# An attention and feed-forward block on one core: when GpSimd adds the residual's bias, where the next input's statistics stand, and which softmax sums VectorE takes

## What is computed

```python
x = x + jnp.tanh(g_xattn[0]) * xattn(_layernorm(x, axis=-1), ctx_2048, wq, bq, wkv, bkv, wp, bp)
x = x + jnp.tanh(g_ffn[0]) * ffn(_layernorm(x, axis=-1), gate_w, up_w, down_w, gate_scale, up_scale, down_scale)
...
q = _qdq(x) @ _qdq(wq).T + bq
kv = cond @ wkv.T + bkv
attn = jax.nn.softmax(jnp.einsum('bnhd,bmhd->bhnm', q, k) * scale, axis=-1)
o = jnp.einsum('bhnm,bmhd->bnhd', attn, v).reshape(B, N, C)
out = _qdq(o) @ _qdq(wp).T + bp
```

## Time and profile before

| | |
|---|---|
| median of three runs | 938.24 us (937.95 to 938.37) |
| the profiled execution, its own time | 936.7 us |
| its span in the profile | 934.9 us |
| PE busy | 864.1 us, 92% |
| DVE busy | 671.5 us, 72% |
| ACT busy | 554.4 us, 59% |
| POOL busy | 256.7 us, 27% |
| granted TensorE clock, mean | 0.991 |

### The profile page before, as it was taken

The page is one execution under the profiler, slowest core; times in us unless marked ns, Lnnn a source line. Parts: engine busy times, 40 slices in busy tenths (PEclk is TensorE's granted clock), DMA queues, the critical chain, the costliest instruction groups (busy, mean ns, idle before and its releaser), DMA issues.

```text
span 934.9 us, 13575 instructions
## 1 busy us (share of the span) xinstructions
PE 864.1 (92%) x5000; PEld 310.2 (33%) x5000; DVE 671.5 (72%) x1292; ACT 554.4 (59%) x693; POOL 256.7 (27%) x236
## 2 busy tenths in 40 slices
PE   5987888999899998999899998999999989998998
PEld 2421121124433331224433331224433322233443
DVE  6887968938676769876766679886867768678222
ACT  5546777562556657884356647885256678871330
POOL 1145789770017603000006713000001213000130
PEclk9998999999999999999999999999999999999999
DMA  9334244410111143200020133210020014200001
GB/s 332 97 89 128 84 125 116 127 46 1 43 32 46 40 125 96 51 2 1 17 58 24 50 109 97 49 32 1 4 48 1 1 46 111 54 1 23 12 1 45
DMA packets 37106, 55.28 MB, mean 59 GB/s; under 512 B 8944, under 2 KB 15152, under 8 KB 37040
## 3 DMA queue, kind: packets, MB, share of 16 engines
q1 hardware_dynamic: 35120, 48.13, 18.1%
q0 software_dynamic: 1920, 6.29, 2.3%
HBM read 31.21 MB, written 4.19 MB: 38 GB/s over the span
## 4 chain that ended last, share of the span: by engine, by line
PE 68%; DVE 13%; ACT 10%; issue 7%; DMA 1%; ACTq 0%; DVEq 0%
PE ps L1325 33%; PE ps L1469 9%; PE ps L1506 8%; PE ps L1486 8%; ACT r L836 5%; PE ps L1448 4%; DVE acc L1080 3%; PE ps L1500 2%; PE ps L1514 1%; PE ps L1309 1%; DVE kst L1055 1%; ACT xq L795 1%; ACT r L795 1%; ACT r L744 1%; DVE r L1222 1%
## 5 line engine op out<-in xcount | busy, mean ns | idle before, releaser
L836 ACT ACTIVATE r<-ps 128x1024 f32<-128x1024 f32 x256 | 251.4, 1022 | 74.1 <-PE ps L1469 71.7
L1469 PE MATMUL ps<-qst,kst 97*128 97x512 f16 x512 | 140.9, 387 | 15.4 <-ACT r L836 13.0
L1055 DVE CUSTOM_DVE_ANT_0 kst<-ps,kst 128x512 f32<-128x512 f32 x192 | 124.5, 686 | 30.3 <-PE ps L1448 28.4
L1486 PE MATMUL ps<-r,vv 128*32 128x512 f32 x1024 | 138.1, 612 | 3.4 <-ACT r L836 3.2
L1080 DVE TENSOR_TENSOR acc<-acc,r 128x1024 f32<-128x1024 f32 x108 | 129.8, 1258 | 3.5 <-ACT r L836 3.1
L795 ACT ACTIVATE kst<-ps 128x1024 f32<-128x1024 f32 x96 | 98.2, 1023 | 53.3 <-PE ps L1381 53.0
L644 POOL TENSOR_TENSOR rstd<-mv,mhalf 128x4 f32<-128x4 f32 x8 | 9.9, 1240 | 344.9 <-DVE mv L966 344.9
L1325 PE MATMUL ps<-xs,w_gate 128*128 128x512 f16 x384 | 91.0, 380 | 1.5 <-DVE xs L1260 1.5
L1325 PE MATMUL ps<-xs,w_up 128*128 128x512 f16 x384 | 91.1, 380 | 0.0
L1469 PEld LDWEIGHTS ps<-qst,kst 97*128 97x128 f16 x512 | 37.6, 98 | 157.4 <-ACT r L836 110.7
L893 ACT ACTIVATE qst<-ps,gs_c 128x512 f32<-128x512 f32 x48 | 33.0, 688 | 67.7 <-PE ps L1325 67.7
(11 more groups left out here) (164 smaller groups left out, 1322.1 us busy)
## 6 DMA issues: line engine op xcount, KB each, us to landing
kst<-k_reg SPq DMA_DIRECT2D x192, 64.0 KB
qst<-q_reg SPq DMA_DIRECT2D x192, 32.0 KB
xs<-in_x SPq DMA_DIRECT2D x4, 1024.0 KB, 6.0
cf<-in_ctxT POOLq DMA_DIRECT2D x16, 256.0 KB, 3.5
xres<-in_x SPq DMA_DIRECT2D x3, 1024.0 KB, 5.4
out<-xres SPq DMA_DIRECT2D x12, 256.0 KB, 2.1
acc<-in_down_w SPq DMA_DIRECT2D x10, 256.0 KB, 2.6
vv<-in_wkvT SPq DMA_DIRECT2D x2, 1024.0 KB, 9.8
```

The lines of the kernel that those rows point to most:

```text
L836: nc.scalar.activation(prob[:, s:s + 2, :], ps[:, first_bank:first_bank + 2, :], ACT.Exp, scale=SCALE).then_inc(exp_done, 1)
L1055: ins = nc.vector.tensor_tensor_reduce(kept(b, n)[:, k, :], bank(PAIR + k), kept(b, n)[:, k, :], 1.0, -3.0e38, ALU.add, ALU.max, mx[:, g % ...
L1469: mm = nc.tensor.matmul(bank(first_bank + k), kst[0:97, g % 2, j + k, t * P:(t + 1) * P], qst[0:97, g % 2, j + k, :], start=True, stop=True)
L1486: mm = nc.tensor.matmul(ps[j * DH:(j + 1) * DH, O_BANK, :], vv[:, t, h * DH:(h + 1) * DH], prob[:, p_slot(b, u, j), :], start=(t == 0), st ...
```

## The change

Three things change. First, for inputs 1 to 3, POOL waits for `den_out` of the same input, which ACT gives behind the last unit, before it adds the bias. Second, of the steps of `x_ahead(2)` and `x_ahead(3)` the four of statistics no longer stand ahead of units 1 to 4 of the following input: two stand beside `DOWN3`, ahead of the last turned maxima, and two behind the last `down_tile`. The step that puts them together moves from unit 5 to unit 3. Third, `ADDED` is now 0 to 6 in all four groups; before, units 11 and 19 had their sums on PE. DVE so covers 28 units of an input where it covered 26, with 24 units' adds where there were 22.

```diff
-AHEAD_UNITS = ((3, 5, 7, 18, 20) + tuple(range(22, 30)), tuple(range(1, 6)) + tuple(range(8, 25)))
+
+AHEAD_UNITS = ((3, 5, 7, 18, 20) + tuple(range(22, 30)), (3,) + tuple(range(8, 25)))
+AHEAD_EARLY = (2, 2)
...
-ADDED = ((0, 1, 2, 3, 4, 5, 6), (0, 1, 2, 4, 5, 6), (0, 1, 2, 4, 5, 6), (0, 1, 2, 3, 4, 5, 6))
+ADDED = (tuple(range(MT - 1)),) * G
...
                     if b < B - 1:
                         inverse_deviation(variance_of_x(b + 1))
+                    pool.wait_ge(den_out, b + 1)
                     residual_bias(b)
...
-                ahead = x_ahead(b + 1) if not last else None
+                if b == 0:
+                    ahead = x_ahead(1)
...
+                ahead = x_ahead(b + 2) if b + 2 < B else None
                 for t in range(NT):
                     name = f"DOWN{t}"
                     if name not in d_seq(b):
                         continue
-                    beside(name)
+                    for part in AHEAD[b].get(name, []):
+                        if part == [("S", G - 1, 0)] and ahead:
+                            for _ in range(AHEAD_EARLY[0]):
+                                next(ahead)
+                        maxima(b + 1, part)
                     down_tile(b, t, b, name)
+                for _ in range(AHEAD_EARLY[1] if ahead else 0):
+                    next(ahead)
```

## The result

| | before | after |
|---|---|---|
| median | 938.31 us (937.95 to 938.67, 4 runs) | 927.22 us (927.07 to 929.05, 4 runs) |
| ratio | | 0.9888, 95% interval 0.9874 to 0.9902 |
| profiled execution, its own time | 936.7 us | 927.18 us |
| its span | 934.9 us | 925.4 us |
| mean granted TensorE clock in it | 0.991 | 0.994 |

The changed kernel is 1.1% faster, 11.1 us from median to median. The two profiled executions lie only 9.5 us apart; where the other 1.6 us come from is taken up under the clock, further down.

A forecast was written before the change was run, and what follows sets the result against it. PE, in step with ACT, was taken to set the pace, waiting 3.43 us for DVE in inputs 1 and 2. Gains of 3.97 us each there and 1.74 in input 3 made 9.68: 938.24 - 9.7 = 928.5 us, range 925.5 to 932.0.

The forecast's parts named there:

- First group: Inputs 1 and 2: with three statistics and the bias gone, PE's wait goes whole and `totals` comes 3.60 us earlier.
- The spare 0.4 us: First group's end, inputs 1 and 2: `totals` could start at 360.86, PE is ready only at 361.29.
- That both parts are needed: First group's end: with bias or statistics moved alone, PE would still wait for the other, 1.4 us or 1.8 us.
- Second and third group: Inputs 1 and 2: DVE wants 19.43 and 18.41 us against PE's 17.43, giving new waits of 2.00 and 0.98.
- the third rival: The change only moves the wait: each step costs some 0.4 us more inside the adds; 936.5 us, chance 0.06.
- Fourth group and input 3: Fourth group: 16.59 us before and after. Input 3: PE's 17.43 sets the pace, two `sums` of 0.87 come out, 1.74.
- What was costed at nothing: Bias behind the units (no collision, at most 0.4 us) and two statistics beside `DOWN3`, in DVE's idle 1.68 us.
- the first rival: The clock falls in the second group, behind the 2.00 us wait; 929.7 to 931.7 us, chance 0.18.
- The mis-sized term: Last step of the sum: the runs' median lies 1.5 us above the profiled execution, so 938.24 is the starting point.
- the price of the fall: Second group, inputs 1 and 2: the clock at half speed behind the first wait lengthens the distance by 1.61 us.

The follow-up runs named there:

- bias_only: The kernel before, with one edit: POOL waits for `den_out` ahead of the bias of inputs 1 to 3; 930.34 us, ratio 0.992.
- without_sums: The changed kernel with `ADDED` as before the change, so the sums of units 11 and 19 are back on PE; 927.85 us, ratio 0.9892.
- added_only: The kernel before, with only the sums changed: DVE adds units 11 and 19 too in inputs 1 to 3; 937.43 us, ratio 0.9995.
- stats_only: The kernel before, with only the early statistics and the new `AHEAD_UNITS`, the bias as it was; 939.65 us, ratio 1.0014.
- bias_at_scaling: The changed kernel, with the bias waiting for the freed bank of O3 in place of `den_out`; 935.28 us, ratio 0.9968.

## Why the prediction was right, point by point

- **First group:** 3.60 us each were forecast. `totals` came 3.29 us earlier in input 1 (364.89 to 361.60) in an execution that was already 0.3 us behind ahead of the units (the wait of the earlier trace rows at 104.03 stands at 104.32), so 3.6. The spare 0.4 us was not there in input 1: DVE's first add came at 347.33, 0.4 us later than forecast even so, and its last ended 0.06 before `totals`. The delay comes with the early statistics: in all six runs that have them this add starts 3.3 us after ACT's first exponential, in the others 3.0. Why is open; input 2 of the changed kernel has 3.0.
- **That both parts are needed** was right for the wait to go whole, wrong for what each does alone. The bias alone leaves 1.27 us, near the 1.4. The statistics alone don't leave 1.8: the wait is 4.14 us in input 1 and 2.73 in input 2, since the bias follows the variance in POOL's queue. The text ahead of the prediction names that queue, and the prediction doesn't ask what an earlier variance would start.
- **Second and third group:** 19.43 and 18.41 were forecast, 19.31 and 18.41 measured. The 0.12 is the last normalising, which I had taken at 0.58. In the kernel before, a reduction stands right behind it, and `x_ahead` lets no reduction start before all four normalisings have ended (`dve.wait_ge(xn_ready, ...)`); now a unit's adds stand between, and it costs 0.46 like the others (369.45 to 369.91). So the third rival's support, a step that costs more inside the adds, was misread. Waits forecast 2.00 and 0.98, measured 1.66 (1.38 in input 2) and 0.77 as the profile counts them, from the end of the matmul before.
- **Fourth group and input 3:** 16.59 and 17.43 forecast, 16.61 and 17.44 measured.
- **What was costed at nothing** cost nothing, but for the late first add above. The bias took 4.96 us, and L1226 beside it kept its 0.68. The two statistics beside `DOWN3` shortened DVE's idle time there from 1.68 to 0.48 us, and the turned maxima weren't late. The Trainium skill (SBUF, "Who interferes with whom") agrees with the runs in both directions: products from PSUM and reductions go free, scalings and adds within SBUF collide.
- **The clock** stayed at 1.00 behind the new waits of 1.66 and 1.38 us, so the first rival didn't come.
- **The mis-sized term** is the last one, "the median of the runs shown lies 1.5 above that execution". Against the profiled execution 927.0 was forecast and 927.18 measured; that they meet to 0.2 us is in part luck, since by distances the gain is 9.8 and the execution happened to be 0.3 us late ahead of the units. But the 1.5 doesn't carry over: the changed kernel's median is its profiled time. I had taken the price of the fall (1.61 us, from one execution) as fixed. Runs of the kernel before beside their mean granted clock show that it isn't:

```
us        clock
935.24    0.993
936.55    0.991
938.65    0.989
940.30    0.987
```

Each step of 0.002 in the clock goes with some 1.7 us (1.3 to 2.1). It is about what one stretch of 3.4 us at half the clock takes off the mean: half of 3.4 over 935 is 0.0018. The kernel before has three long waits (two of 3.43 us, and one of 2.56 near the end, which all versions here keep), and around each of them the clock may be low for 3.4 or for 6.8 us. The last one can also pass without a fall; the same wait of 2.55 us, the matmuls behind it in two versions:

```profile
857.30:864.10 6.80, 4.81 (x30) 3.08 (x31) 3.64 (x6) 2.74 (x5) 0.00 (x0) 1.00 0.10 39
855.00:861.80 6.80, 5.30 (x17) 2.46 (x16) 2.69 (x5) 1.99 (x5) 0.00 (x0) 0.50 0.10 39
```

The first row is `bias_only`, the second `without_sums`. Counted in stretches of 3.4 us around these three waits, the traces have none in `bias_only` (mean clock 0.996), one in the changed kernel (0.994), two in `without_sums` (0.993), three in the kernel before (0.991), four in `added_only` (0.989) and five in `stats_only` (0.987). The median run of the kernel before had 0.989, which by this count is one stretch more than its profiled execution, and that accounts for the 1.6 us (11.1 less 9.5). At which of the three waits it lay isn't seen in an execution without a trace.

Of the gain, by distances: the bias's place 7.5 us (in each of two inputs 2.16 off the first wait and some 1.57 off the distance behind it), the statistics on top of it 2.9 (the distance from input 1's fourth `totals` to input 2's first goes from 159.41 in `bias_only` to 157.97 in `without_sums`), and the sums lose 0.5: 1.7 gained in input 3 and 2.2 given back in inputs 1 and 2. That is 9.8 us (the terms are rounded), and the 9.5 of the profiled executions is this less the 0.3 us of lateness. The medians (938.10 for the kernel before beside these runs, then 930.34, 927.85, 927.22) say 7.8, 2.5 and 0.6 gained for the same three, with the clock's falls mixed in.

## What to carry to other kernels

Cost an edit in the unit in which two engines meet (here from `totals` to `totals`), once for each engine, and take the larger; the same edit then has its right sign in each place. When a producer moves forward, read on in its consumer's queue: whatever stands behind starts earlier too, and may land on a busier neighbour. A long stall on PE can be dearer than its length and scatter the measurement, so compare clocks before comparing medians.

## What the runs showed of the hardware

- DVE's adds with two inputs in SBUF and its scalings and normalisings within SBUF collide with POOL's additions, its reductions and its products from PSUM don't: seven adds against the bias took 12.33 us in place of 8.0, and the four additions 8.42 in place of 4.96; four reductions beside the same additions took 2.46. One POOL addition of 1.27 us costs DVE about 1.1 us, whether an add of 128x1024 or a TENSOR_SCALAR on 128x4 (0.17 to 1.29) stands against it; a scaling that met only the end of one lost 0.74 (0.49 to 1.23).
- The same wait doesn't always bring the same clock: around 2.98 us it fell once and stayed once in the same execution, around 3.43 us it was low for 3.4 or for 6.8 us, and around the 2.56 us near the end it fell in seven of the nine traces and stayed in two. At the 2.73 us of `stats_only` it fell. From 100 us on it stayed behind every wait of PE of 1.98 us or less that had no longer one just ahead of it; in `bias_at_scaling` the fall near the end came 1.2 us behind a wait of 1.98 us, which itself followed the one of 2.55 by 2 us. The Trainium skill (TensorE: Matmul & The Clock Gate, "HAM oscillation") speaks of idle gaps over some 3.4 us; the traces disagree in that 2.56 us could be enough.
- The longest wait doesn't tell the whole: in all nine traces the clock is low for 6.8 us in input 0, from 76 to 79 us on, with no single wait over 1.22 us near it. Ahead of this fall PE was busy in the changed kernel for 1.38 of 3.40 us:

```profile
73.20:76.60 3.40, 1.38 (x10) 0.33 (x10) 2.88 (x10) 2.67 (x5) 1.78 (x2) 1.00 0.83 257
76.60:83.40 6.80, 5.05 (x18) 0.72 (x18) 3.43 (x9) 4.02 (x5) 3.70 (x4) 0.50 0.73 205
```
